# Seven tiles of the second mean from gathered edge rows, and an attention tail in three 16-bit parts

## The reference

```python
edge_index = jnp.stack([src, dst])
h = jnp.maximum(_layernorm(x, axis=-1), 0.0)
x = x + _L0_gnn_ref(h, edge_index, W1, b1, W2, b2, a)      # hypergraph convolution, twice
h = jnp.maximum(_layernorm(x, axis=-1), 0.0)
x = x + _L1_gnn_ref(h, relvectors, ..., src, dst, edge_type_16)   # messages, then a GRU cell
h = jnp.maximum(_layernorm(x, axis=-1), 0.0)
x = x + _L2_gnn_ref(h, edge_index, W, b, gamma, beta)      # graph convolution, norm
h = jnp.maximum(_layernorm(x, axis=-1), 0.0)
x = x + _L3_gnn_ref(h, edge_index, weight, attn_l, attn_r) # attention over 4 heads
# _hconv, used twice in L0
m = segment_sum(xt[src], dst) / count(dst)          # mean over the edges of a dst node
out = segment_sum(m[dst], src) / count(src) + b
# L3: only the first n edges are used; alpha is a softmax over the 4 heads
alpha = softmax(leaky_relu(alpha_l[row] + alpha_r[col], 0.01), axis=1)
tmp = einsum('nh,nhd->nd', alpha[:n], xt[col[:n]]); out = tmp repeated for each head
```

## Time and profile before

| | us |
|---|---|
| median of three runs | 1314.7 (1312.56 to 1317.72) |
| the profiled execution, its own time | 1314.68 |
| span of the trace | 1312.9 |
| PE busy | 1238.3 (94%) |
| DVE, ACT, POOL busy | 687.8, 441.3, 161.2 |
| mean granted PE clock | 0.979 of full |

### The profile page before, as it was taken

The page is one execution under the profiler, slowest core; times in us unless marked ns, Lnnn a source line. Parts: engine busy times, 40 slices in busy tenths (PEclk is TensorE's granted clock), DMA queues, the critical chain, the costliest instruction groups (busy, mean ns, idle before and its releaser), DMA issues.

```text
span 1312.9 us, 23447 instructions
## 1 busy us (share of the span) xinstructions
PE 1238.3 (94%) x9553; PEld 976.5 (74%) x9553; DVE 687.8 (52%) x1874; ACT 441.3 (34%) x937; POOL 161.2 (12%) x338
## 2 busy tenths in 40 slices
PE   1699999989999999999999999999999998999994
PEld 1466666768999986666888887777776777889893
DVE  7866556764555744333355541453444556555626
ACT  2755554447676621111111121222221221122203
POOL 6710000220000000000111110000000112111200
PEclk9999999999999999999999999999999999999957
DMA  4100000013111111000444320111110121000003
GB/s 166 70 25 1 1 1 1 1 45 128 51 64 52 51 57 44 0 0 1 135 155 169 127 99 17 37 37 37 37 37 26 40 82 65 22 21 21 17 1 100
DMA packets 38600, 67.10 MB, mean 51 GB/s; under 512 B 4586, under 2 KB 23191, under 8 KB 38356
## 3 DMA queue, kind: packets, MB, share of 16 engines
q1 hardware_dynamic: 33872, 53.59, 12.0%
q10 hardware_dynamic: 4132, 10.63, 2.3%
q0 software_dynamic: 480, 1.30, 0.4%
HBM read 38.95 MB, written 26.56 MB: 50 GB/s over the span
## 4 chain that ended last, share of the span: by engine, by line
PE 86%; DVE 6%; ACT 3%; POOL 1%; DMA 1%; issue 1%; DVEq 0%; ACTq 0%
PE ps L467 38%; PE ps L1862 11%; PE ps L756 10%; PE ps L1886 4%; PE ps L723 3%; PE ps L817 3%; PE ps L819 3%; PE ps L712 3%; PE ps L843 2%; PE ps L823 2%; PE ps L821 2%; PE ps L789 1%; PE ps L876 1%; POOL st L679 1%; PE ps L883 1%
## 5 line engine op out<-in xcount | busy, mean ns | idle before, releaser
L467 PE MATMUL ps<-big,pairB 125*128 125x250 fp8e4 (+1 forms) x2600 | 302.9, 267 | 0.6 <-DVE big L1181 0.6
L467 PEld LDWEIGHTS ps<-big,pairB 125*128 125x128 f16 x2600 | 238.7, 98 | 30.1 <-issue 2.8
L1862 PE MATMUL ps<-pairA,adj 125*125 125x512 f16 x625 | 207.0, 404 | 0.0
L679 POOL TENSOR_TENSOR st<-st,mhalf 125x1 f32<-125x1 f32 x100 | 61.4, 614 | 865.8 <-DVE st L1276 865.8
L467 PE MATMUL ps<-adj,pairB 125*128 125x250 fp8e4 (+1 forms) x1300 | 147.3, 269 | 1.8 <-DVE pairB L1334 1.8
L467 PE MATMUL ps<-adj,pairA 125*128 125x250 fp8e4 (+1 forms) x1300 | 139.2, 268 | 0.0
L467 PEld LDWEIGHTS ps<-adj,pairB 125*128 125x128 f16 x1300 | 124.1, 99 | 17.1 <-DVE pairB L1334 2.0
L756 PE MATMUL ps<-pairA,adj 125*125 125x512 f16 x625 | 135.2, 380 | 0.0
L467 PEld LDWEIGHTS ps<-adj,pairA 125*128 125x128 f16 x1300 | 120.8, 98 | 19.3 <-issue 7.7
L1799 ACT ACTIVATE adj<-ps 125x450 fp8e4<-125x450 f32 (+6 forms) x191 | 97.3, 518 | 102.2 <-PE ps L1888 101.8
L1888 PEld LDWEIGHTS ps<-wih 128*128 128x128 bf16 x615 | 84.6, 144 | 51.9 <-issue 0.8
(11 more groups left out here) (276 smaller groups left out, 1708.2 us busy)
## 6 DMA issues: line engine op xcount, KB each, us to landing
t_adjTp<-big SPq DMA_DIRECT2D x25, 400.0 KB, 2.4
big<-t_adjTp ACTq DMA_DIRECT2D x25, 400.0 KB, 4.1
t_xh<-work SPq DMA_DIRECT2D x13, 256.0 KB, 2.0
pairB<-in_x SPq DMA_DIRECT2D x5, 640.0 KB, 11.2
t_h0p<-pairB SPq DMA_DIRECT2D x5, 640.0 KB, 2.9
work<-t_xh SPq DMA_DIRECT2D x25, 128.0 KB, 2.3
xin<-t_xh SPq DMA_DIRECT2D x25, 128.0 KB, 2.3
xin<-t_x2p SPq DMA_DIRECT2D x25, 128.0 KB, 2.0
```

The costliest lines, as they stand in the source:

```text
L467: last = pe.matmul(out, src[:, j, FEAT * part + 128 * c:FEAT * part + 128 * (c + 1)], rhs(j, p), start=(j + part == 0 and not begun), stop ...
L679: g.tensor_tensor(st[:, 9:10], st[:, 8:9], k.mhalf[:, 0:1], ALU.pow).then_inc(S[rstd], 1)
L1862: last = pe.matmul(k.ps[0:P, 6 + t % 2, :], k.adj[:, j, PITCH * i:PITCH * i + P], k.pairA[:, j, :], start=(j == 0), stop=(j == TILES - 1))
```

## The change

1. **Second mean.** Tiles 18 to 24 (`SPARSE` = 7) no longer use 25 dense matmuls each. The rows of `pairA` are stored to memory (`store_g`, 25 DMAs on SP's queue, each behind `keep(i)`), and POOL gathers the source rows of up to 10 slots of 128 edges per tile (`GATHERS` = 70 indirect DMAs, 1 KB for each of 128 edges), into a ring of 12 buffers that is refilled four at a time. PE multiplies each with a one-hot of the edge's destination (`far_mean2`, 10 matmuls of 512 columns a tile; DVE makes the one-hots in `far_hots`). The tiles are taken in the order 4 dense, 1 gathered, 3, 1, 2, 1, 2, 1, 3, 1, 2, 1, 2, 1. The load of `w_hhT` moves behind `load_xh(1)`.
2. **Build.** A sixth group of slots (`ALL` = GROUPS + 1) gives the sources and destinations of these edges: one gather of each kind more, one row of `starts`, 640 in place of 512 columns in `keys`, one `turn_keys` more.
3. **Tail.** The f32 operands of the one-hot matmuls are split in three bf16 parts that add up to them exactly (`thirds_of`), and each pick is three bf16 matmuls. The search for alpha_l is cut in three portions of tiles (`PARTS`): 150 matmuls stand inside the graph convolution (`FINDS`), 75 behind it. Rows of z are copied from PSUM by ACT (`far_out`) as they come, 7 of 13 pairs ahead of the softmax and the rest between the groups of the last loop (`LATER`). The sum over heads goes from DVE to PE (`sum_heads`, four f32 matmuls of 256 columns a group).

```diff
+SPARSE, EACH = 7, 10
+DENSE = TILES - SPARSE
+GATHERS = SPARSE * EACH
+AHEAD = 4
...
+    PARTS = ((0, 8), (8, 17), (17, TILES))
+    SUMS = (4, 0)
+    FINDS = [(6, 10), (6, 34), (10, 30), (11, 6)]
+    LATER = [(7,), (8, 9), (10, 11), (12,), (), (), ()]
...
+        def store_g(i):
+            sp.wait_ge(A["lo"], i + 1)
+            sp.dma_start(rows(d["pairs"], i), k.pairA[:, i, :]).then_inc(M["stored"], 16)
...
+            if i >= 6:
+                store_g(i - 6)
...
         load_xh(0)
         load_xh(1)
+        sp.dma_start(k.whh[:, :, :], d["w_hhT"].rearrange("(c f) n -> f c n", f=128)).then_inc(W["whh"], 16)
...
+        pool.wait_ge(M["stored"], 16 * TILES)
+        for s in range(GATHERS):
+            if s >= DEEP and s % AHEAD == 0:
+                pool.wait_ge(F["used"], s - DEEP + AHEAD)
+            g.indirect_dma_start(ring[s % DEEP], None, d["pairs"], bass.IndirectOffsetOnAxis(ap=k.far_src[:, s:s + 1], axis=0)
+                                 ).then_inc(landed(s)[0], 16)
...
+        def far_mean2(t):
+
+            if t >= 4:
+                pe.wait_ge(M["t"], t - 3)
+            s0 = EACH * (MEAN_ORDER[t] - DENSE)
+            for s in range(s0, s0 + EACH):
+                pe.wait_ge(F["hot"], s + 1)
+                if s == s0 or s % AHEAD == 0:
+                    pe.wait_ge(*landed(s))
+                last = pe.matmul(k.ps[0:P, t % 4, :], far_hot[s % DEEP], ring[s % DEEP], start=(s == s0), stop=(s == s0 + EACH - 1))
+                last.then_inc(F["used"], 1)
...
+        def pick_thirds(out, hot, parts):
+
+            for n, part in enumerate(parts):
+                last = pe.matmul(out, hot, part, start=(n == 0), stop=(n == 2))
+            return last
+
+        def find(n, bank, free):
+
+            part, half = divmod(n, 2)
+            a, b = PARTS[part]
+            pe.wait_ge(T["halves"], part + 1)
+            pe.wait_ge(T["hot"], 1)
+            pe.wait_ge(*free)
+            w = HEADS * (b - a)
+            for t in range(13 * half, min(13 * half + 13, TILES)):
+                at = w * (t - 13 * half)
+                last = pick_thirds(k.ps[0:P, bank, at:at + w].rearrange("p (h t) -> p h t", t=b - a), equal(t), [x[:, :, a:b] for x in left_third])
+            last.then_inc(T["found"], 1)
...
+        def pick_z(f):
+
+            pe.wait_ge(*((T["copied"], f - 1) if f >= 2 else (C["copied"], NP - 1) if f else (C["read"], TILES - 1)))
             for t in range(2 * f, min(2 * f + 2, TILES)):
-                last = pe.matmul(k.ps[0:P, FAR[f % len(FAR)], FEAT * (t % 2):FEAT * (t % 2 + 1)], chosen(t), z[0][:, 0:FEAT],
-                                 start=True, stop=True)
+                last = pick_thirds(k.ps[0:P, 3 if f % 2 else 5, FEAT * (t % 2):FEAT * (t % 2 + 1)], chosen(t), [x[:, 0:FEAT] for x in z_third])
             last.then_inc(T["far"], 1)
...
+        def sum_heads(n):
+
+            t0, t1 = QUADS[n]
+            pe.wait_ge(T["weighed"], n + 1)
+            if t1 - t0 > 2:
+                pe.wait_ge(T["scaled"], n + 1)
+            pe.wait_ge(*((T["done"], n - 1) if n >= 2 else (C["turned_out"], TILES) if n else (C["read"], TILES)))
+            for h in range(HEADS):
+                last = pe.matmul(k.ps[0:P, SUMS[n % 2], 0:DH * (t1 - t0)].rearrange("p (t c) -> p t c", c=DH), k.ident[:, 0:P],
+                                 scaled[n % 2][:, 0:t1 - t0, DH * h:DH * (h + 1)], start=(h == 0), stop=(h == HEADS - 1))
+            last.then_inc(T["summed"], 1)
...
+        pick_z(2)
+        find(4, 7, (T["picked"], 4))
+        find(5, 2, (C["copied"], NP - 2))
+        for f in range(3, 7):
+            pick_z(f)
+        for n in range(len(QUADS)):
+            sum_heads(n)
+            for f in LATER[n]:
+                pick_z(f)
...
+        def far_out(f):
+
+            t1 = min(2 * f + 2, TILES)
+            act.wait_ge(T["far"], f + 1)
+            s.copy(far_z[:, 2 * f:t1, :], k.ps[0:P, 3 if f % 2 else 5, 0:FEAT * (t1 - 2 * f)].rearrange("p (t c) -> p t c", c=FEAT)
+                   ).then_inc(T["copied"], 1)
+
+        far_out(0)
+        far_out(1)
         rest(TILES - 1)
+        for f in range(2, 7):
+            far_out(f)
         act.wait_ge(T["shifted"], 1)
         s.activation(al[:, :, :], al[:, :, :], ACT.Exp).then_inc(T["raised"], 1)
         act.wait_ge(T["weights"], 1)
...
                 last.then_inc(T["scaled"], 1)
+            for f in LATER[n]:
+                far_out(f)
...
+        def thirds_of(parts, rest, x, ready):
+
+            own.link(v.tensor_copy(parts[0], x))
+            own.link(v.tensor_tensor(rest, x, parts[0], ALU.subtract))
+            own.link(v.tensor_copy(parts[1], rest))
+            v.tensor_tensor(parts[2], rest, parts[1], ALU.subtract).then_inc(ready, 1)
...
+        def halves(a, b):
+
+            dve.wait_ge(C["z"], b)
+            thirds_of([x[:, :, a:b] for x in left_third], rest_left[:, :, a:b], left[:, :, a:b], T["halves"])
...
+        def far_hots(i):
+
+            s0 = EACH * (i - DENSE)
+            for s in range(s0, s0 + EACH):
+                if s >= DEEP:
+                    dve.wait_ge(F["used"], s - DEEP + 1)
+                v.tensor_scalar(far_hot[s % DEEP], k.far_iota[:, 0:P], k.far_rows[:, 1, s:s + 1], 1.0 / CNT, ALU.is_equal, ALU.mult,
+                                saturate=False).then_inc(F["hot"], 1)
...
+            if i in (9, 18):
+                halves(*PARTS[i // 10])
+            if i in (10, 11, 19, 20):
+                pick((10, 11, 19, 20).index(i), 7)
...
+        dve.wait_ge(T["found"], 5)
+        own.link(v.tensor_tensor(a, a, k.ps[0:P, 1, 0:TILES * HEADS].rearrange("p (t h) -> p t h", h=HEADS), ALU.add))
+        halves(*PARTS[2])
...
+        pick(4, 7)
+        pick(5, 2)
...
+        def weigh(n):
+            t0, two = QUADS[n][0], min(2, QUADS[n][1] - QUADS[n][0])
+            dve.wait_ge(T["copied"], 2 * n + 1)
+            if n >= 2:
+                dve.wait_ge(T["summed"], n - 1)
+            v.tensor_tensor(scaled[n % 2][:, 0:two, :].rearrange("p t (h c) -> p t h c", h=HEADS),
+                            far_z[:, t0:t0 + two, :].rearrange("p t (h c) -> p t h c", h=HEADS),
                             a[:, t0:t0 + two, :].unsqueeze(3).to_broadcast([P, two, HEADS, DH]), ALU.mult).then_inc(T["weighed"], 1)
...
+        def add_far(n):
+            t0, t1 = QUADS[n]
+            x = k.x3[:, t0:t1, :].rearrange("p t (h c) -> p t h c", h=HEADS)
+            dve.wait_ge(T["summed"], n + 1)
+            v.tensor_tensor(x, x, k.ps[0:P, SUMS[n % 2], 0:DH * (t1 - t0)].rearrange("p (t c) -> p t c", c=DH)
+                            .unsqueeze(2).to_broadcast([P, t1 - t0, HEADS, DH]), ALU.add).then_inc(T["done"], 1)
...
+        weigh(0)
+        weigh(1)
+        for n in range(len(QUADS)):
+            add_far(n)
+            if n + 2 < len(QUADS):
+                weigh(n + 2)
...
+            dve.wait_ge(near_in[min(a, 1)], 16 * (b - a))
             for g in range(a, b):
-                dve.wait_ge(near_in[g], 16)
...
-            for n in range(a, b):
-                dve.wait_ge(edges_in[n], 16)
+            dve.wait_ge(edges_in[min(a, 1)], 16 * (b - a))
...
+            if b > GROUPS:
+                v.tensor_scalar(hi_key[:, GROUPS, :], raw[:, GROUPS, :, 0], 0.0, None, ALU.max)
...
-                starts(1, GROUPS)
+                starts(1, ALL)
             if m == 8:
-                keys(1, GROUPS)
+                keys(1, ALL)
```

336 lines of the change are left out of this document (171 added, 165 removed).

## The result

| | before | after |
|---|---|---|
| median of 4 runs, us | 1314.91 (1312.56 to 1317.72) | 1333.18 (1326.87 to 1335.45) |
| the profiled execution, its own time | 1314.68 | 1335.45 |
| span of the trace | 1312.9 | 1333.3 |
| ratio to before | | 1.0126, 95% interval 1.0108 to 1.0145 |

What follows compares the result with a forecast made beforehand. PE, busy for 94% of the span, was taken as the bound. Build +6, second mean -10, graph convolution +7, tail to the weights -7.5 and last loop +14.5 gave +10, so 1325 us, range 1311 to 1338.

Steps and rivals of the forecast that it cites:

- Build, +6: Build: 3.9 us longer wait for the keys, 0.6 transposes, 1.5 half clock; 6 us more, bounds 3 and 8.
- The wait at `turn_keys`: Build: sign of the step, PE's wait at the first `turn_keys` behind slot 72 near 4.6 us.
- Second mean, -10: Second mean: 22.8 us of matmuls saved, less 9.8 of waits for gathers and 3 of half clock; 10 us saved.
- if the stores came 2 us late: Second mean: risk that late stores of the rows to gather would cut the saving by as much.
- if gathers start further apart: Second mean: sign that the prediction is wrong; it took gathers on POOL to start 1.25 us apart.
- POOL sets the second mean: Second mean: rival with gathers 1.6 us apart, costing 4 us instead of saving 10; 1339 us, chance 0.13.
- Convolution, +7: Graph convolution: 150 searches at 53 ns add 8.0 us, `one_hots` gives back 1 to 2, clock dips cost 0.5.
- The working's lower price, 25 ns: Graph convolution: lower end for one search matmul, from the 9-column L1888; 150 would cost 3.8 us.
- Tail to the weights, -7.5: Last `dense_c` to softmax weights: 32.6 us at half clock, table load on the path, against 40.5; 7.5 us saved.
- the rival that it holds: Tail: rival that PE's clock stays full, tail 49.2 us instead of 61.4; 1306 us, chance 0.12.
- Last loop, +14.5: Last loop: 35.4 us with a switching clock, against 20.9; 14.5 us more, bounds +6 and +21.
- the ring named: Last loop: ACT scales, PE sums, PE picks, ACT copies, then ACT scales again; 5.45 or 8.5 us per two-pick group.

Runs made afterwards that it cites:

- e5: Changed kernel with the four 400 KB reloads of `load_at(0)` and `load_at(1)` sent eight tiles later on ACT's queue: 1327.2 us, ratio 1.0087.
- e4: Changed kernel with the ring of gathered rows refilled in twos (six semaphores) in place of fours, same 12 buffers: 1326.0 us, ratio 1.0086.
- e6: Changed kernel with the edits of e4 and e5 and the first gathered tile two tiles later (gaps 6, 2, 2, 2, 2, 2, 2): 1325.1 us, ratio 1.0067.
- e3: Changed kernel with the sum over heads back on DVE, two additions a group, and all late picks in one row on PE: 1316.3 us, ratio 1.0014.
- e2: Changed kernel with PE's picks of `LATER[n]` placed ahead of the sum of group n in the last loop: 1319.5 us, ratio 1.0034.
- e8: Changed kernel with the sixth group's steps in the build moved behind bulks 9 and 12: 1329.9 us, ratio 1.0127.
- e9: Changed kernel with all mends: twos, later reloads, six gathered tiles, later sixth group, `right` in five pieces, picks first, early table load and exponential: 1296.3 us, ratio 0.9860.
- e10: e1 with picks ahead of sums, so build and second mean as before the change: 1315.7 us, ratio 0.9995 to the kernel before.
- e1: Changed kernel without the sixth group, stores, gathers and `far_mean2`, so the change's tail alone: 1331.8 us, ratio 1.0141 to the kernel before.

## Why the prediction was right or wrong

**Total.** 1333 lies in the range, 8 us above the forecast. The direction and the largest loss were right; one term was far off: the second mean missed its -10 by 9.6 us. That the time stayed inside the range is in part luck, since the build came out 2.5 us cheaper than forecast and the median lies 2.3 us below the profiled execution.

**Build, +6.** Measured +3.5 in the profile and 4.2 as the mean of all profiles. The counts' delay (they start +1.4 for +1.25, and one more took 0.3 as said) and the keys' length (5.9 us, +1.2 for +1.1) followed the working. The keys end +3.06 for +3.9 later: the last gather landed sooner (3.0 us after its start, 4.15 before). What failed is adding the half clock and the wait. The wait at `turn_keys` that was to show the step, near 4.6 us, is 0.29. The clock fell ahead of the keys, at a wait for `bulk(7)` that I had not named, and the slow matmuls filled time in which PE would have waited for the keys anyway.

**Second mean, -10.** The step that failed. 22.8 us for 105 matmuls was right; the waits were 16.3 us and not 9.8 (7.8 for 5.2 at the first gathered tile, 5.4 for 3.5 at the third, 3.1 for 1 at the last two), and clock and rest took 6.1 and not 3. Three terms of it were mis-sized. The stores: "about 494" for the last one supposed 3 us of landing, and they took 6.3 because `load_at` left at the same moment; that was named as a risk ("if the stores came 2 us late") but I did not look at what else leaves then. It cost 8.4 us (`e5`). The refilling in fours: counted, but with too little weight; it cost 10.2 us (`e4`). The spacing: 1.25 us is what an undisturbed gather needs, and the sign named for being wrong ("if gathers start further apart") came true: the first 20 were 1.33 us apart on average. All 21 gathers with DVE idle beside them took 0.94 or 0.95 us. Of the other 49, 22 took under 1.00 and the rest up to 1.77, and all nine over 1.2 us stand beside `overlay` (L1348), an operation of the kernel before that the working left out. The two single gains are not to be added: both together gave 12.7 (`e6`). The rival "POOL sets the second mean" had the right mechanism with a smaller spacing than its 1.6 us; the end of the stage in `e6` shows it at work. (By the Trainium skill, *SBUF — State Buffer*, section "SBUF: two separate sides", operations of DVE that hold the shared port keep GpSimd from writing DMA descriptors; the lengths of 0.95 and 1.77 agree with that, though no run here takes `overlay` out.)

**Behind the mean, 0.** The wait of 2.77 us at the last gathered tile left the clock at half in `back2`: +1.3. I had forecast no wait there. It does not always cost that: with waits of 2.31, 2.35 and 1.72 us at the same place `e3`, `e4` and `e5` kept the clock at 1.00 behind it and the old length of the stage (445.05 us from `back2` to the next layer's matmuls, 446.3 in the changed kernel), while 2.36 and 2.40 us (`e2`, `e8`) lowered it. `e9`, which ends on a dense tile and does not wait there, has the old length too.

**First convolution, 0.** +1.6, by the clock at 0.57 from 301 to 305 us, behind a wait of 2.22 us that stands in both kernels. In the twelve profiles of this study the stage takes either 198.3 us (the kernel before, `e4`, `e9`, `e10`) or 200.0 (the other eight, `e1` with the old build and no stores among them). So it is a dip that comes or not; whether the stores of the change make it likelier is open.

**Convolution, +7.** Measured +5.8. A search of 39 matmuls, and the one behind it:

```profile
1158.21 2.38 PE L927 MATMUL ps<-whh,CT 125*125 125x32 bf16 x39
1160.44 1.02 PE L478 MATMUL ps<-adj,pairB 125*128 125x250 fp8e4 x8
```

That is 57 ns a matmul, as L712, where I took 53: 8.6 us for 150. PE's wait at 1106 us is down from 2.12 to 1.01 us:

```profile
1111.56 0.43 PE L912 MATMUL ps<-ident,work 125*128 125x125 f32 x2 [1.01 <-ACT work L1145]
```

The half clock behind it did not come (1.00 from 1110 to 1117). Together they gave back 2.7 us, where I took 1 to 2. No dip followed the searches. The working's lower price, 25 ns, came from L1888, whose weights have 128 columns. In the earlier trace rows that is read at half clock, though the stretch view gives 1.00 there; the pair does take 0.21 us there and 0.13 at 215 us. Later in the kernel before, the reading is plain:

```profile
215.15 0.18 PE L1888 MATMUL ps<-wih 128*128 128x9 bf16 x1
215.18 0.26 PE L1886 MATMUL ps<-whh,Wg 128*128 128x225 fp8e4 x1
```

L1888 holds PE for 28 ns (the median of 504), half of the 57 that a search takes with 125 columns of weights. It stands behind a wide matmul, though, and a search behind a short one, so the two compare only roughly. (The 25 ns that the Trainium skill gives for 32 columns, *TensorE: Matmul & The Clock Gate*, section "Wait — 56ns, not 53.3ns?", does not hold for matmuls that each load 125 columns of weights: 57 ns with 32 and with 36 columns, 58 with 4. With 128 columns the 28 ns of L1888 agree with it.)

**Tail to the weights, -7.5.** Measured -7.6. The clock was at half from 1257 on (0.53 in 1257 to 1260, 0.50 in 1260 to 1279), as the working had it, and the rival that it holds did not come. The table load stood on the path behind the copies. `right` took 7.1 us, as forecast.

**Last loop, +14.5.** Measured +15.4, and by the ring named: `e2` cuts it and the loop is 21.2 us. The groups with two picks took 7.7 and 5.9 us, between the two ends of 5.45 and 8.5; those with one took 7.0 and 5.3. One term was off: scaling takes 2.02 us for eight operations that read SBUF, where 1.74 was taken from ones that read PSUM.

**The misses together.** The forecast was 8 us low in all: -2.5 for the build, +9.6 for the second mean, +2.9 for clock elsewhere, -1.2, -0.1, +0.9 and +0.8 for the rest make +10.4 in the profiled execution, which was the slowest of four; the median is 2.3 us lower.

## What to carry to other kernels

When an engine gets a new step between two others, write down the ring (who waits for whom until the same engine is ready again) and ask whether the order inside it can be turned: one swapped pair of lines was worth 14 us here. A gathered operand is only as fast as its refilling: count when the first and the last request can go, in what portions buffers come free, and what else is on the DMA engines when the data that the gathers read is stored. Ask too what another engine does beside each request, since a neighbour's long operation stretched the gathers here. And put short matmuls in small pieces between wide ones, and avoid a wait at the end of a stage: behind five of eight such waits PE's clock was at half.
